# A threshold search in a two-block attention and expert kernel: ScalarE counts two PSUM banks in one instruction, VectorE's accumulator starts from a constant

## What is computed

```python
N, E = 2048, 8
k = int(CAPACITY_FACTOR * N / E)                         # 256
route_prob = jax.nn.softmax(xf @ Ws + bs, axis=-1).T     # 8 x 2048
route_vals, routes = jax.lax.top_k(route_prob, k)
xin = xf[routes]
h = jax.nn.gelu(jnp.einsum('ekd,edf->ekf', xin, W1) + b1[:, None, :])
out = jnp.einsum('ekf,efd->ekd', h, W2) + b2[:, None, :]
out = out * route_vals[..., None]
final = jnp.zeros((N, D), dtype=x.dtype).at[routes.reshape(-1)].add(out.reshape(-1, D))
```

## Time and profile before

| | |
|---|---|
| runs, median (lowest to highest) | 218.1 us (218.04 to 218.97) |
| profiled execution, span from first to last instruction | 215.8 us |
| TensorE matmul busy | 182.6 us, 85% |
| VectorE busy | 132.5 us, 61% |
| ScalarE busy | 90.3 us, 42% |
| GpSimd busy | 101.6 us, 47% |
| mean granted TensorE clock | 0.988 of full speed |

### The profile page before, as it was taken

The page is one execution under the profiler, slowest core; times in us unless marked ns, Lnnn a source line. Parts: engine busy times, 40 slices in busy tenths (PEclk is TensorE's granted clock), DMA queues, the critical chain, the costliest instruction groups (busy, mean ns, idle before and its releaser), DMA issues.

```text
span 215.8 us, 3590 instructions
## 1 busy us (share of the span) xinstructions
PE 182.6 (85%) x1231; PEld 110.0 (51%) x1236; DVE 132.5 (61%) x456; ACT 90.3 (42%) x219; POOL 101.6 (47%) x111
## 2 busy tenths in 40 slices
PE   6888997988999978999999997888879878988740
PEld 2544542344434545376776764332358666866630
DVE  5787889257874889676689788888846311101110
ACT  2423772342722574146644453558535302333210
POOL 0599648000244021811147498200367787888632
PEclk9999999999999999999999999999999999999995
DMA  6625212101100001079810202100022223332312
GB/s 177 195 70 151 71 51 55 33 22 48 30 3 0 0 0 49 5 256 308 267 54 0 84 21 100 52 0 0 9 60 26 38 38 44 45 37 39 37 23 29
DMA packets 16127, 13.64 MB, mean 63 GB/s; under 512 B 3699, under 2 KB 13079, under 8 KB 16103
## 3 DMA queue, kind: packets, MB, share of 16 engines
q1 hardware_dynamic: 12246, 10.61, 16.3%
q0 software_dynamic: 2944, 2.30, 7.9%
q10 hardware_dynamic: 913, 0.43, 0.8%
HBM read 8.02 MB, written 3.21 MB: 52 GB/s over the span
## 4 chain that ended last, share of the span: by engine, by line
PE 39%; DVE 25%; POOL 13%; issue 9%; DMA 6%; ACT 3%; POOLq 1%; DVEq 0%
POOL out L1947 7%; PE psum L1011 7%; DVE mrow L1527 5%; DMA out<-pT,idx 5%; DVE pT L1673 4%; PE psum L1029 3%; DVE stats L1409 3%; PE psum L918 3%; POOL pT L1939 2%; PE psum L908 2%; DVE le L1724 2%; PE psum L981 2%; PE psum L1092 2%; PE psum L952 2%; PE psum L1048 2%
## 5 line engine op out<-in xcount | busy, mean ns | idle before, releaser
L1837 POOL TENSOR_SCALAR ve<-mv 128x4 f32<-128x4 f32 (+1 forms) x19 | 4.4, 231 | 70.5 <-DVE mv L1412 70.3
L775 ACT ACTIVATE pT<-psum 103x512 f32<-103x512 f32 (+1 forms) x36 | 21.2, 596 | 30.2 <-PE psum L983 30.2
L1947 POOL DMA_INDIRECT out<-pT,idx x16 | 25.5, 1594 | 10.4 <-DVE pT L1741 7.0
L1939 POOL DMA_INDIRECT pT<-gather_rows,idx x16 | 17.2, 1073 | 22.7 <-DVE idx L1728 18.7
L1527 DVE TENSOR_REDUCE mrow<-psum 128x8 bf16<-128x616 f32 x32 | 24.6, 788 | 5.1 <-PE psum L952 5.1
L908 PE MATMUL psum<-c 128*128 128x512 bf16 x103 | 26.5, 379 | 1.2 <-ACT key_map L800 1.0
L1739 DVE TENSOR_TENSOR pT<-psum,b_rows 128x256 f32<-128x256 f32 (+1 forms) x9 | 3.5, 394 | 35.3 <-PE psum L1365 35.3
L1353 PE MATMUL psum<-xinT,w 128*128 128x256 f32 (+1 forms) x72 | 16.2, 368 | 4.5 <-ACT xinT L860 3.6
L1554 DVE RECIPROCAL rden<-psum 128x512 f32<-128x512 f32 (+1 forms) x5 | 13.6, 2715 | 6.7 <-PE psum L1011 6.0
L865 ACT ACTIVATE pT<-psum,b 128x256 f32<-128x256 f32 (+1 forms) x36 | 14.3, 451 | 7.7 <-PE psum L1353 7.7
L1365 PE MATMUL psum<-w,pT 128*128 128x128 f32 x128 | 17.1, 283 | 0.2 <-DVE flag L1747 0.2
(11 more groups left out here) (201 smaller groups left out, 376.3 us busy)
## 6 DMA issues: line engine op xcount, KB each, us to landing
w<-in_L_ffn_W SPq DMA_DIRECT2D x16, 256.0 KB, 5.7
gather_rows<-xrow SPq DMA_DIRECT2D x4, 272.0 KB, 2.1
x<-in_x SPq DMA_DIRECT2D x4, 256.0 KB, 4.5
q_stack<-q_hi SPq DMA_DIRECT2D x32, 32.0 KB, 1.8
out<-res SPq DMA_DIRECT2D x4, 256.0 KB, 2.1
q_stack<-q_lo SPq DMA_DIRECT2D x24, 32.0 KB, 1.8
b_rows<-in_L_ffn_b SPq DMA_DIRECT2D x1, 512.0 KB, 3.7
pT<-gather_rows,idx POOLq DMA_INDIRECT x16, 2.7
```

Source lines behind the costliest of these rows:

```text
L775: nc.scalar.activation(pT[0:n, b % 2, s, :], ST_ps[s % 2][0:n, :], ACT.Exp).then_inc(exp_done, 1)
L1939: nc.gpsimd.indirect_dma_start(xin[:, e, h, :], None, gather_rows, bass.IndirectOffsetOnAxis(idx[:, h, e:e + 1], 0), bounds_check=last_row ...
L1947: nc.gpsimd.indirect_dma_start(flat, bass.IndirectOffsetOnAxis(idx[:, h, e:e + 1], 0), y[:, e, h, :], None, bounds_check=last_row, oob_is_ ...
```

## The change

The images of batches 2 and 3 both stay in PSUM, in banks 5 and 4, next to each other; the image of batch 2 was in bank 6 before and was copied out. ScalarE takes the signs over both banks with one instruction and has one sum. VectorE's count gives a constant as second operand beside the accumulated sum, `ACT_T * T / 2 - CAP + 0.25`, with which the accumulator begins; the separate instruction that doubled and added is gone, and the compare forms 2 x count and compares it with ScalarE's sum. The state of the search shrinks from seven to five columns.

```diff
-        spread = pT[:, 0, 5:5 + B - 1, :]
+        spread = pT[:, 0, 5:5 + ACT_T, :]
-        search_state = sb("search_state", [P, 7])
-        found, low, mark = search_state[:, 0:4], search_state[:, 4:5], search_state[:, 5:7]
+        search_state = sb("search_state", [P, 5])
+        found, low, mark = search_state[:, 0:2], search_state[:, 2:3], search_state[:, 3:5]
...
-        spread_ps = [bank[7], bank[7], bank[6], bank[4]]
+        spread_ps = [bank[7], bank[7], bank[5], bank[4]]
+        counted_ps = psum[:, 4:6, :]
...
-            spread_out(t)
             share_exp(B - 1, ua, a0, a1)
             share_exp(B - 1, ub, b0, b1_)
-            act.wait_ge(spread_done, B - 1)
             act.wait_ge(spread_ps_done, UNITS)
             for i in range(LEVELS):
                 act.wait_ge(mark_done, i + 1)
-                nc.scalar.activation(marks[:, 1, 0:T], spread[:, B - 2, :], ACT.Sign, bias=mark[:, i % 2:i % 2 + 1], scale=-1.0, accum_out=found[:, 2:3])
-                nc.scalar.activation(marks[:, 1, T:2 * T], spread_ps[B - 1], ACT.Sign, bias=mark[:, i % 2:i % 2 + 1], scale=-1.0,
-                                     accum_out=found[:, 3:4]).then_inc(act_count_done, 1)
+                nc.scalar.activation(marks[:, 1, :].rearrange("p (b t) -> p b t", b=ACT_T), counted_ps, ACT.Sign, bias=mark[:, i % 2:i % 2 + 1],
+                                     scale=-1.0, accum_out=found[:, 1:2]).then_inc(act_count_done, 1)
...
                     if i == 0:
-                        pe.wait_ge(spread_done, B - 1)
+                        pe.wait_ge(spread_done, ACT_T)
...
-                        settle(dve.tensor_scalar(marks[:, 0, :], spread[:, 0:B // 2, :].rearrange("p b t -> p (b t)"), at, None, ALU.is_ge, ALU.add,
-                                                 accum_out=found[:, 0:1]))
-                        settle(dve.tensor_scalar(found[:, 1:2], found[:, 0:1], 2.0, ACT_T * T - 2.0 * CAP + 0.5, ALU.mult, ALU.add))
+                        settle(dve.tensor_scalar(marks[:, 0, :], spread.rearrange("p b t -> p (b t)"), at, ACT_T * T / 2 - CAP + 0.25, ALU.is_ge,
+                                                 ALU.add, accum_out=found[:, 0:1]))
                         dve.wait_ge(act_count_done, i + 1)
-                        dve.scalar_tensor_tensor(enough[:], found[:, 2:3], found[:, 3:4], found[:, 1:2], ALU.add, ALU.is_le).then_inc(ge_done, 1)
+                        dve.scalar_tensor_tensor(enough[:], found[:, 0:1], 2.0, found[:, 1:2], ALU.mult, ALU.is_ge).then_inc(ge_done, 1)
```

## The result

| | kernel before | changed kernel |
|---|---|---|
| first comparison, median (lowest to highest), 4 runs each | 218.53 us (218.04 to 219.9) | 216.07 us (215.77 to 216.27) |
| ratio, 95% interval | | 0.9878 (0.9836 to 0.992) |
| profiled span | 215.8 us | 214.4 us |
| mean granted TensorE clock | 0.988 | 0.988 |

The forecast was a ratio of 216.5 / 218.1 = 0.993, and its range began at 215.9 / 218.1 = 0.990. The direction was right, the range was missed on the side of the gain. Taken by itself, the time of 216.07 us lies inside the stated 215.9 to 217.5; but the kernel before, timed beside it, took 218.53 us and not the 218.1 from which the forecast was counted.

A forecast was written before the change was run, and what follows sets the result against it. The bound was the search, one serial loop of six levels, about 14 us. Per level 0.20 + 0.07 us saved, 1.6 over six, gave span 214.2, plus 2.3 kept 216.5 us, 0.73% less; range 215.9 to 217.5.

The forecast's parts named there:

- line 1675 and its hand-over gone: VectorE in each search level: removing the instruction that doubles and adds, with its semaphore hand-over, saves 0.20 us.
- constant in the accumulator: VectorE's count, line 1673: starting from a constant costs 0; rival of 0.15 us per level, 217.4 us, chance 0.06.
- ScalarE's instruction over two banks: ScalarE in each level: one ACTIVATE of 1024 elements takes 1.09 us; rival that ScalarE becomes the bound, 217.7, chance 0.04.
- ScalarE's slack: Ahead of the compare, line 1677: ScalarE would allow its start at 144.53, VectorE at 144.62, so 0.09 us to spare.
- TensorE's idle time ahead of the matmul: In front of line 1295, behind eight warming matmuls: 0.27, 0.28, later 0.42 us, becoming 0.00, 0.01, later 0.15.
- what the edges cost: First two search levels, TensorE's warming matmuls and VectorE's probT copy: together 0 to 0.17 us lost once, taken as 0.
- cover for VectorE's: ScalarE's arm in each level: ends 0.30 us earlier, worth next to nothing by itself, but lets VectorE's shortening count.
- VectorE a little later: Two arms meeting at line 1677, nearly level: with only one shortened, the other holds the level after some 0.05 us.
- those 2.3 kept: Whole kernel: the median run, 218.1 us, lies 2.3 above the profiled span; kept, the forecast is 216.5 us.
- some 0.2 of run spread: Whole kernel: allowance around the forecast beside the edges' 0 to 0.17 us, giving 216.2 to 216.9 with chance 0.72.
- The tail: Rival after the search: scatters meet DMA landings at another phase, 0.3 to 1.0 us more or less; chance 0.10.
- the rule weighed: A semaphore between VectorE instructions costs nothing extra; the removed instruction is then worth 0.08 per level, the sum 0.9 us.

The follow-up runs named there:

- all runs at equal clock: The fit of one slope and one step to 98 runs of the kernel before and 26 of the changed kernel: 2.3 us per 0.01 of mean clock, 1.63 us quicker.
- the two one-sided kernels: Two kernels: the changed one with VectorE's steps as before, ratio 0.9992; the changed one with an extra ScalarE copy per level, search 13.37 us.
- its filled twin: The kernel before with eight unused matmuls in TensorE's idle time at about 33.5 us; ratio 0.9973 to the kernel before.
- its twin: The changed kernel with eight unused matmuls in TensorE's idle time at about 33 us; ratio 0.9932, repeated 0.9903, to the kernel before.
- the version meant to be quicker: The changed kernel with each mark formed from the last, `low` only at the end; search 12.1 us; with idle time filled and seven warming matmuls, ratio 0.991.

## Why the prediction was right, and where it was wrong

The terms, one by one:

| term | forecast | measured |
|---|---|---|
| line 1675 and its hand-over gone | 0.20 per level | compare starts 1.32 behind the count, was 1.53: 0.21 |
| constant in the accumulator | 0 | 1278 ns, was 1280 |
| compare with a constant | 0.07 | 161 ns, was 222; the matmul starts 0.22 behind its start, was 0.28: 0.06 |
| ScalarE's instruction over two banks | 1.09 us | 1.11 us |
| ScalarE's slack | 0.09 | 0.18 less the 0.10 that the hand-over takes: 0.08 |
| TensorE's idle time ahead of the matmul | 0, 0, then 0.15 | none in the first three levels, then 0.16 |
| what the edges cost | 0 (0 to 0.17) | first two pitches 2.08 and 2.04: 0 |
| the search | 1.6 less | 13.91 to 12.32: 1.59 less |
| all runs at equal clock | 1.6 less | 1.63 less, standard error 0.23; 1.49 of it in the span |

So the mechanism of the level and every size in it held. ScalarE's part was called cover for VectorE's, worth next to nothing alone, and that is what the two one-sided kernels showed. What I didn't say is how exactly the arms met before: I read ScalarE's 0.11 as a gap with some slack in it, and it was the whole hand-over. "VectorE a little later" was the wrong way round, by 0.01, and the 0.05 that it gave a one-sided change was 0.02 for the one side and 0.07 for the other.

The step that failed is what the sum carried over from the kernel before as if it were fixed: "So span 215.8 - 1.6 = 214.2", "with those 2.3 kept", and around it "some 0.2 of run spread", taken from three runs of 218.04 to 218.97 and one profile. The runs showed in its place:

- The kernel before took 218.53 in the comparison, 0.43 above the 218.1 of the forecast. It ran between 216.2 and 225.2 us in 98 executions, and with four runs on each side the comparison had an interval of 0.8%, 1.8 us.
- The changed kernel took 216.07, 0.43 below the forecast. Its median lay 1.7 us above its profiled span where 2.3 was kept, 0.6 less; against that its span was 214.4 and not 214.2.
- That span held 1.59 less of search, 1.06 less of head and 1.2 more of tail. Over the fourteen profiles the search began anywhere from 135.2 to 140.3 and the tail took 61.0 to 63.5, in both kernels and their variants, while the length of the search was 13.90 to 13.91 in three profiles of the kernel before and its filled twin, and 12.32 to 12.34 in five of the changed one and its twin.

So the 2.5 us of the comparison hold 1.6 of the search and 0.9 that no instruction of the change makes. The tail was a rival, with 0.10 for its phase; the head wasn't named at all, because nothing in it was changed, and the time outside the span was named and held fixed. That a part isn't changed says nothing of its spread.

By the rule weighed, the Trainium skill's page "VectorE: DVE Perf Modes", section "The DRAIN you can't avoid", the search would have gained 0.9 us; the measured 1.59 decides for the row. The Trainium skill measured that a semaphore costs nothing extra on eight copies, of 13.88 us together; for VectorE instructions of 0.15 us a wait in between costs. The removed instruction with its wait gave back 0.21, and one without a wait, the update of `low` in the version meant to be quicker, 0.07.

What stays open: why the kernel before was slow in the first comparison. By the fit above, the changed kernel should take 216.1 us at the mean clock of its four runs, 0.989, and took 216.05 in the mean. So, as an estimate, the excess lies in the four runs of the kernel before, of which only the profiled one's clock is known; 0.984 in the mean would account for their 218.75. Open too are what makes q_lo early or late, why the tail varies, why the time outside the span is 0.1 shorter in the changed kernel, and why the clock falls in one execution and not in the next behind the same idle time.

## What to carry to other kernels

Where two engines work side by side and meet, compare the end of each plus its own hand-over with the start of what waits: if both come out at that start, shortening one gives next to nothing, and the two edits have to be made together. In VectorE's instructions here, a constant in the accumulator or as an immediate was free, and a number that stood as a column in SBUF cost 62 ns each time. And judge an edit of less than 1% by the length of its own stretch in the profile, since that repeated within 0.02 us here while the runs spread over 9.

## What the runs showed of the hardware

- A handed-over result costs more from ScalarE than within VectorE: the compare started 0.10 us behind ScalarE's accumulator read, and 0.03 behind VectorE's own.
- Around an idle time of TensorE of 0.95 us the clock fell to 1.2 GHz, for 3.4 or 10.2 us, in eight of ten profiles of kernels whose TensorE had the same work up to there, and not in the other two; with that time filled, in none of four. Falls of 3.4 us made that part of the kernel 1.2 to 1.8 us longer, 10.2 us made it about 4.5 longer.
- An ACTIVATE of 1024 elements out of two adjacent PSUM banks took 1114 ns, 447 more than one of 512 out of one bank (667 ns, to the hundredth), 0.87 ns per element. Inside one bank the slope was 0.82 (line 865 of the kernel before: 474 ns for 256 elements, 369 for 128) to 0.84 (line 700: 583 for 512, 368 for 256). So the step into the second bank cost 0.02 to 0.03 us.
